# Last tile of a fused attention, recurrence and mixture-of-experts kernel: three rectifications on VectorE, a second bank for the transposes, new orders behind the last step

## What is computed

```python
a = cond_attention(x, cond)             # 16 heads, softmax over heads
x = x + linear_attention(a)             # cumulative over the heads of a token
# gated recurrence, one step per token s, all 32 batches side by side
fused = sigmoid(concat[x_s, h] @ w_W + w_b); hidden_state, output_state = split(fused, 2)
memory = x_s @ wx_W + wx_b + hidden_state * (h @ wh_W + wh_b)
h = output_state * h + (1 - output_state) * tanh(memory)
# mixture of experts over all h: 8 experts of 128 hidden units, the top 2 of 8 weighted
hidden = square(relu(einsum('nc,ecd->ned', h, w1_all)))
out    = sum over the top 2 of softmax(top-2 logits) * (hidden @ w2_all)
x = x + out
```

## Time and profile before

| | us |
|---|---|
| median of 3 runs | 379.13 |
| the 3 runs | 374.61, 379.13, 379.33 |
| the profiled execution, its own time | 374.6 |
| its span, first to last instruction | 372.9 |
| mean granted clock of TensorE in it | 0.999 |

### The profile page before, as it was taken

How to read it: one execution, slowest core, us unless ns; L and a number is a source line. 1 busy time by engine, 2 the same in 40 slices (tenths; PEclk the granted TensorE clock), 3 DMA queues, 4 the chain that set the end, 5 groups by cost and what they waited for, 6 DMA issues and landing times.

```text
span 372.9 us, 9070 instructions
## 1 busy us (share of the span) xinstructions
PE 358.7 (96%) x2528; PEld 301.9 (81%) x2528; DVE 319.2 (86%) x1160; ACT 292.6 (78%) x1136; POOL 258.2 (69%) x272
## 2 busy tenths in 40 slices
PE   6999999989999999999999999999999999999985
PEld 5689788658888888888888888888888888888873
DVE  3467897999999999999999999999999999998530
ACT  3555445568898999998999999899999989877764
POOL 4898341688777777777777777777777777777000
PEclk9999999999999999999999999999999999999999
DMA  7500000000000000000000000000000000000000
GB/s 237 202 2 0 4 0 3 0 3 1 9 10 8 10 7 11 10 11 10 10 8 10 9 9 9 8 10 8 9 8 10 8 11 9 9 9 7 10 9 14
DMA packets 7442, 6.76 MB, mean 18 GB/s; under 512 B 736, under 2 KB 6112, under 8 KB 7392
## 3 DMA queue, kind: packets, MB, share of 16 engines
q1 hardware_dynamic: 6816, 5.84, 5.0%
q10 hardware_dynamic: 576, 0.35, 0.3%
HBM read 4.09 MB, written 2.10 MB: 17 GB/s over the span
## 4 chain that ended last, share of the span: by engine, by line
PE 78%; DVE 13%; issue 4%; ACT 2%; DMA 1%; ACTq 0%; DVEq 0%; POOL 0%
PE bank L388 68%; PE bank L532 7%; DVE kvs L1095 3%; DVE mem L1135 1%; DMA XT<-in_x_t_dram 1%; PE bank L434 1%; DVE att L1104 1%; DVE rden L1087 1%; PE bank L489 1%; DVE h L1155 1%; DVE CTX L1023 1%; DVE bank L1147 1%; PE bank L481 1%; DVE bank L1140 1%; DVE ssub L1008 1%
## 5 line engine op out<-in xcount | busy, mean ns | idle before, releaser
L345 POOL TENSOR_TENSOR qc<-kvs,qn 128x512 f32<-128x512 f32 x64 | 81.4, 1273 | 53.1 <-DVE kvs L1095 52.7
L388 PEld LDWEIGHTS bank<-h,gwh 128*128 128x128 f32 x512 | 67.7, 191 | 20.8 <-DVE h L1155 16.8
L333 POOL TENSOR_TENSOR kv<-kv,qkv 128x512 f32<-128x512 f32 x64 | 80.0, 1273 | 0.2
L1095 DVE TENSOR_TENSOR_SCAN kvs<-bank,kv 128x256 f32<-128x256 f32 x128 | 79.7, 665 | 0.4 <-POOL kv L333 0.3
L840 ACT ACTIVATE hid<-bank,gw 128x128 f32<-128x128 f32 x256 | 76.8, 371 | 3.1 <-ACT gw L862 0.4
L388 PE MATMUL bank<-h,gwh 128*128 128x32 f32 x512 | 72.3, 264 | 3.5 <-DVE h L1155 3.4
L388 PE MATMUL bank<-rw,h 128*128 128x392 f32 (+2 forms) x192 | 74.9, 472 | 0.0
L388 PE MATMUL bank<-w,hsq 128*128 128x128 f32 x512 | 64.5, 279 | 0.7 <-ACT hsq L850 0.7
L388 PEld LDWEIGHTS bank<-w,hsq 128*128 128x128 f32 x512 | 59.9, 192 | 1.4 <-ACT hsq L850 1.4
L388 PE MATMUL bank<-h,whw 128*128 128x64 f32 x256 | 53.0, 289 | 0.0
L869 ACT ACTIVATE gt<-bank 128x64 f32<-128x64 f32 x128 | 29.9, 233 | 25.5 <-PE bank L388 24.3
(11 more groups left out here) (113 smaller groups left out, 704.2 us busy)
## 6 DMA issues: line engine op xcount, KB each, us to landing
out_dram<-res SPq DMA_DIRECT2D x32, 64.0 KB
XT<-in_x_t_dram SPq DMA_DIRECT2D x7, 256.0 KB, 5.3
rw<-in_rw_dram SPq DMA_DIRECT2D x1, 516.0 KB, 5.2
w<-in_w_dram SPq DMA_DIRECT2D x1, 512.0 KB, 5.9
XT<-in_x_t_dram ACTq DMA_DIRECT2D x1, 256.0 KB, 5.0
aw<-in_aw_dram SPq DMA_DIRECT2D x1, 192.0 KB, 4.2
gwx<-in_gw_dram SPq DMA_DIRECT2D x1, 128.0 KB, 4.6
gwh<-in_gw_dram SPq DMA_DIRECT2D x1, 128.0 KB, 4.4
```

What stands on the lines that cost most here:

```text
L333: pool.tensor_tensor(kv[:, a * D:b * D, :].rearrange("p (d e) h -> p d e h", d=D // 2), kv[:, D * D + a:D * D + b, :].unsqueeze(2).broadca ...
L345: pool.tensor_tensor(qc[:, a:b, :, :], kvs[:, a * D:b * D, :].rearrange("p (d e) h -> p d e h", d=D // 2), qn[:, p, a:b, :].unsqueeze(2).b ...
L388: return pe.matmul(dst, w, rhs, start=start, stop=True, skip_group_check=True)
L1095: dve.tensor_tensor_scan(flat(kvs[:, a:b, :]), scan_mask, flat(kv[:, a:b, :]), 0.0, ALU.mult, ALU.add).then_inc(kv_sum, 1)
```

## The change

Only the last tile and the finales are touched.

- DVE gets a `relu` of its own: experts 3 (half 0) and 4, 5 (half 1) of tile 31, each one `tensor_scalar` from the bank MEM into `hid`, multiplied by a column of `gw` and then the maximum with 0. It waits for `hidden` piece 1 and for `gw`, and it counts a new semaphore `hid_dv`. ACT keeps experts 0, 1, 2, 6 and 7, and `hid_sb` now counts after expert 2 and after expert 7. `hidden_T(31, half)` waits for both semaphores.
- `turned_bank`: the transposes of half 1 of tile 31 go to QKV rather than TR, and `hidden_T(31, 1)` no longer waits for `square(31, 0)`.
- `hidden(31, piece 2)` no longer waits for `hid_b`.
- PE's finale: x_rows(30), hidden_T(30, 0), hidden(31, 0), hidden_T(30, 1), experts_out(30, 0), experts_out(30, 1), hidden(31, 1), x_rows(31), hidden(31, 2), hidden_T(31, 0), hidden_T(31, 1), experts_out(31, 0), experts_out(31, 1).
- ACT's finale: x_rows_out(30), square(30, 0), square(30, 1), gate_exp(31), relu of 0 to 2, taken_sum(31), finish(30), x_rows_out(31), relu of 6 and 7, square(31, 0), square(31, 1), finish(31).
- DVE's finale: the three logit operations of tile 31, taken_inverse(30), taken_inverse(31), relu of 3, relu of 4 and 5.

```diff
--- before.py
+++ after.py
@@ -167,6 +167,7 @@
 
         l_top, l_out, l_dl, gw_done, gs_done, gr_done, mask_ok = (
             sem(n) for n in ("l_top", "l_out", "l_dl", "gw_done", "gs_done", "gr_done", "mask_ok"))
+        hid_dv = sem("hid_dv")
         hid_ps, hid_a, hid_b, hid_sb, hT_ps, hsq_sb, o_ps = sem("hid_ps"), sem("hid_a"), sem("hid_b"), sem("hid_sb"), sem("hT_ps"), sem("hsq_sb"), sem("o_ps")
 
         XTt = XT[:, :, :].rearrange("p b t -> p t b")
@@ -215,6 +216,9 @@
         def hidden_bank(t, piece):
 
             return (QKV, MEM, HID)[piece] if is_last(t) else HID
+
+        def turned_bank(t, half):
+            return QKV if is_last(t) and half else TR
 
         def out_bank(t):
             return Z if is_last(t) else OUT
@@ -519,7 +523,7 @@
                     at_least(pe, hid_sb, 2 * t)
                 if piece == 1 and not is_last(t):
                     pe.wait_ge(hid_a, t + 1)
-                if piece == 2:
+                if piece == 2 and not is_last(t):
                     pe.wait_ge(hid_b, t + 1)
                 if t == 0:
                     pe.wait_ge(pT_sb, 2 * QUADS)
@@ -527,9 +531,12 @@
 
             def hidden_T(t, half):
                 pe.wait_ge(hid_sb, 2 * t + half + 1)
-                at_least(pe, hsq_sb, 2 * t + half)
+                if is_last(t):
+                    pe.wait_ge(hid_dv, half + 1)
+                if not (is_last(t) and half):
+                    at_least(pe, hsq_sb, 2 * t + half)
                 for j in range(4):
-                    last = pe.transpose(TR[:, j * P:(j + 1) * P], hid[:, half, j, :], ident[:, :])
+                    last = pe.transpose(turned_bank(t, half)[:, j * P:(j + 1) * P], hid[:, half, j, :], ident[:, :])
                 last.then_inc(hT_ps, 1)
 
             def experts_out(t, half):
@@ -690,18 +697,18 @@
                     hidden(t - 1, q, 2)
 
             def finale():
+                x_rows(30, 0)
                 hidden_T(30, 0)
-                x_rows(30, 0)
-                x_rows(31, 1)
                 hidden(31, 1, 0)
                 hidden_T(30, 1)
                 experts_out(30, 0)
                 experts_out(30, 1)
                 hidden(31, 1, 1)
+                x_rows(31, 1)
+                hidden(31, 1, 2)
                 hidden_T(31, 0)
-                hidden(31, 1, 2)
+                hidden_T(31, 1)
                 experts_out(31, 0)
-                hidden_T(31, 1)
                 experts_out(31, 1)
 
             pipeline(pe, ramp, iteration, finale, 3)
@@ -839,15 +846,15 @@
                     col = NE + e * DE - PIECES[piece][0]
                     last = act.activation(hid[:, half, e - 4 * half, :], hidden_bank(t, piece)[:, col:col + DE], ACT.Relu,
                                           scale=gw[:, p, NE - 1 - e:NE - e])
-                    if e in (2, 5):
+                    if e in (2, 5) and not is_last(t):
                         last.then_inc({2: hid_a, 5: hid_b}[e], 1)
-                    if e in (3, 7):
+                    if e in ((2, 7) if is_last(t) else (3, 7)):
                         last.then_inc(hid_sb, 1)
 
             def square(t, half):
                 act.wait_ge(hT_ps, 2 * t + half + 1)
                 at_least(act, o_ps, 2 * t + half - 1)
-                act.activation(hsq[:, half, :], TR[:, :], ACT.Square).then_inc(hsq_sb, 1)
+                act.activation(hsq[:, half, :], turned_bank(t, half)[:, :], ACT.Square).then_inc(hsq_sb, 1)
 
             def taken_sum(t, p):
 
@@ -960,8 +967,8 @@
                     relu(t - 1, q, 1, 1)
 
             def finale():
+                x_rows_out(30)
                 square(30, 0)
-                x_rows_out(30)
                 square(30, 1)
                 gate_exp(31, 1)
                 relu(31, 1, 0, 0)
@@ -969,10 +976,8 @@
                 taken_sum(31, 1)
                 finish(30, 0)
                 x_rows_out(31)
-                relu(31, 1, 0, 2)
-                relu(31, 1, 1, 0)
+                relu(31, 1, 1, 1)
                 square(31, 0)
-                relu(31, 1, 1, 1)
                 square(31, 1)
                 finish(31, 1)
 
@@ -1103,6 +1108,17 @@
                     at_least(dve, aT_ps, t)
                 dve.tensor_reduce(att[:, :, a:b].rearrange("p h e -> p e h"),
                                   qc[:, 0:D // 2, a:b, :].rearrange("p d e h -> p e h d"), AX.X, ALU.add).then_inc(a_red, 1)
+
+            def relu(t, p, half, some):
+                experts = {(0, 2): (3,), (1, 0): (4, 5)}[half, some]
+                dve.wait_ge(hid_ps, 3 * t + 2)
+                dve.wait_ge(gw_done, t + 1)
+                at_least(dve, hT_ps, 2 * t + half - 1)
+                for e in experts:
+                    col = NE + e * DE - PIECES[1][0]
+                    last = dve.tensor_scalar(hid[:, half, e - 4 * half, :], hidden_bank(t, 1)[:, col:col + DE], gw[:, p, NE - 1 - e:NE - e], 0.0,
+                                             op0=ALU.mult, op1=ALU.max)
+                last.then_inc(hid_dv, 1)
 
             def largest_logits(t):
 
@@ -1275,11 +1291,13 @@
                     sum_heads(t + 2, 3)
 
             def finale():
-                taken_inverse(30, 0)
                 largest_logits(31)
                 drop_others(31)
                 less_top(31)
+                taken_inverse(30, 0)
                 taken_inverse(31, 1)
+                relu(31, 1, 0, 2)
+                relu(31, 1, 1, 0)
 
             pipeline(dve, ramp, iteration, finale)
 
```

## The result

| | before | after |
|---|---|---|
| median of 20 runs each, us | 376.70 | 374.62 |
| lowest run, us | 374.61 | 372.22 |
| ratio of after to before, 95% interval | | 0.9942 (0.9925 to 0.9958) |
| span of the profiled execution, us | 372.9 | 373.5 |
| mean granted clock in it | 0.999 | 0.994 |

The change makes the kernel 0.58% faster, 2.1 to 2.2 us. One of the 20 executions before took 589.21 us, slow and far out of line, and has no part in the ratio. The spans of the two profiled executions say nothing on it: all that the change touches lies behind the last h, and up to there the execution of after happened to be 2.7 us later (why is told at the end). So the measure from here on is the distance from the end of the last h (the scan of DVE that writes `h`) to the start of `finish(31)` (ACT, `res`).

A forecast was written before the change was run, and what follows sets the result against it. The finale was taken to be set by waits from engine to engine, not one engine's load. Front 0.73 + back 1.50 = 2.23 us, taken from the median 379.13, gave 376.9 us (0.994); range 372.0 to 378.8.

The forecast's parts named there:

- all four waits: PE's finale: waits for x_rows_out(30), for expert 3, for square(31, 0), and late square(31, 1); all touched by the change.
- The front: From last h to the end of piece 1: x_rows(30) and x_rows_out(30) first, hidden(31, 0) starts earlier; gain 0.73 us.
- a restart: Four PE transposes take 0.67 us after a wait, 0.44 without; hidden_T(30, 1) forecast as one, ending at 361.12.
- E: The end of piece 1, hidden(31, 1), on PE; forecast at 363.63, before 364.36.
- The back: From the end of piece 1 to finish(31): start moves from 5.27 to 3.77 us behind it; gain 1.50 us.
- Rival 1: DVE's rectifications bound the second half, at 0.55 us each; gain 1.7 us, 377.4 us; chance 0.08.
- rival 2: The front does not move, hidden_T(30, 1) or the logits being the real wait; gain 1.7, 377.4 us; chance 0.08.
- rival 3: ACT's order takes the back's gain, x_rows_out(31) delaying what queues behind; gain 1.4 to 1.7, 377.6 us; chance 0.12.
- rival 4: Slower: DVE's operation on a bank holds hidden_T(31, 1); at 1.5 us each 380.3 us; chance 0.02.
- rival 5: Another wait, the store or one unnamed, holds the end; gain under 0.5 us, about 379.0 us; chance 0.03.
- two levels, 374.6 and 379.1 to 379.3: Whole executions: one earlier run at the lower level, two at the upper; one in four put on the lower.
- The chances by 2%: Whole kernel: faster by over 2% 0.01, within 2% 0.98, slower by over 2% 0.01.

The follow-up runs named there:

- the run with the square first: Kernel after, with square(30, 0) ahead of x_rows_out(30) on ScalarE and hidden_T(30, 0) ahead of x_rows(30) on PE; 7.80 us from last h to finish(31).
- the version above: On the run with the square first, PE runs pieces 1, 2 and x_rows(31) before experts_out(30, 0), rectifications moved earlier; 7.16 us from h to finish(31), ratio to before 0.9924.
- the back alone: Kernel after with the finale's front order put back as before; VectorE's rectifications, second bank and back order stay; 8.66 us from last h to finish(31), ratio 0.9941.
- VectorE's share given back: Kernel after with experts 3, 4 and 5 back on ScalarE ahead of x_rows_out(31); 8.40 us from last h to finish(31), ratio 0.9909.
- work doubled: Kernel after with each VectorE rectification done twice, first into a spare tile nobody reads; 8.41 us from last h to finish(31).
- one bank: Kernel after with both transposed halves in TR, hidden_T(31, 1) waiting for square(31, 0) again; 8.48 us from last h to finish(31), ratio 0.9944.
- the front alone: Kernel before with only the front's reordering, no VectorE rectification, one transpose bank, old back order; 9.46 us from last h to finish(31), ratio 0.9972.
- the old one: Kernel after with the back's old order on PE and ScalarE, VectorE's rectifications and second bank kept; 9.36 us from last h to finish(31), ratio 1.0006.
- the fill: The version above plus two unread 256-column matmuls between step_memory(1, 1, 1) and step_gates(1, 1, 2) in PE's ramp; median 373.30 us, ratio to the kernel before 0.9904.

## Why the prediction was right, and where it was off

**The gain.** The forecast was 2.23 us, a ratio of 0.994; measured were 2.08 us in the profiles and 0.9942 in the times. The mechanism and its places were right, all four waits went, and the one wait that was forecast to stay, for expert 7, is the one left.

**The front.** Forecast 0.73, measured 0.69. Piece 0 ended 0.97 after h (forecast 0.94), `hidden_T(30, 1)` at 1.57 (1.52), E at 4.07 (4.03). Its inner step, that the square comes later by one ACT operation and makes the transposes a restart, was right too: 0.60 rather than 0.44 on the chain, and the run with the square first gives the 0.16 back. I counted this step as part of the forecast and did not draw the conclusion that the swap itself is a loss.

**The back.** Forecast 1.50, measured 1.38; E to `finish(31)` 3.89 us rather than 3.77. The term that was mis-sized is the last `experts_out`, "E + 1.90 to E + 3.75" with no gap. It took 1.95 rather than 1.85: `square(31, 0)` ended at E + 1.75 (forecast 1.69), only 0.17 before `hidden_T(31, 1)` did, which is too late for PE to load the first weights under the transposes. The loads show it: PE's first load for `experts_out(31, 0)` starts at 368.18, 0.05 behind the square, and in the version above it starts 0.27 before the transposes end. Six profiles give the price. Where the square ends 0.05 us before the transposes (the back alone) the 16 matmuls take 2.07, at 0.17 they take 1.95, at 0.23 (VectorE's share given back) 1.90, and at 0.44 and more (work doubled, one bank, the version above) 1.86. In the first three, lead and duration add up to 2.12 to 2.13, so the square has to be done about 2.12 - 1.86 = 0.26 us ahead to cost nothing (an estimate from these rows). The forecast had it 0.21 ahead and took that for enough. The other 0.02 are small shifts of ACT.

**VectorE's rectifications.** The estimate from the neighbouring forms was 339 ns; they take 344 ns, three in 0.87. That it came within 5 ns is partly luck, since its slope was taken from another operation. They ended at E + 0.91 (forecast 0.95), 0.31 before expert 7 (forecast 0.24). Rival 1 had the right shape: with the work doubled the loss is 0.45 and its threshold is where the rows put it. The rule of the Trainium skill (VectorE: DVE Perf Modes, The DRAIN you can't avoid) that the next operation waits for the pipe to empty is, taken alone, not what the rows show: 3 x 0.344 would be 1.03, and six in the doubled run start every 0.26. The prediction left out how that section goes on: a next operation that is not held starts earlier. With that the trace agrees. For ACT, two rectifications took 0.62 again, not the 0.68 that was estimated from the Trainium skill (ScalarE: Activation LUTs, What ACT_TABLE_LOAD costs).

**The other rivals.** The front moved (rival 2), as the front alone shows. ACT's order did not take the back's gain (rival 3): `x_rows_out(31)` started at E + 0.14 and was over before piece 2 ended. Nothing was slower (rival 4), and nothing foreign held the end (rival 5).

**The absolute time.** 376.9 us was forecast, 374.6 measured, inside the range but 2.3 off. The step that failed is the one that took the three runs of before for "two levels, 374.6 and 379.1 to 379.3" and put the median on the upper one. With 20 runs the median of before is 376.7, and the times in between are filled. 376.7 - 2.23 = 374.5 would have been the forecast from it. Three runs do not place a median that moves by 5 us between executions. The chances by 2% were right.

**What the forecast missed** is that the kernel after the change still had 0.8 us on the table, in the same few lines: its own sum held eight transposes in 1.35 us (E + 0.55 to E + 1.90; measured 1.36) that are 0.88 of work, because of the wait for expert 7, and a restart in the front. An order with the pieces first removes 0.48 there, 0.16 in front, 0.09 in the last 16 matmuls, and 0.09 because the pieces and the 16 matmuls of tile 30 take 2.87 rather than 2.96; that is 0.80 but for rounding.

## What to carry to other kernels

Behind the last step of a pipeline, write the chain as a list of hand-overs (PE to ACT to PE) and give each engine something else to do in each; an offload or an extra buffer is worth little until the order lets the engines overlap (here 0.44 and 0.52 us in the new order, 0.10 together in the old one). Let a result be ready some 0.3 us before PE wants it, not just in time (1.86 rather than 1.95 to 2.07 us for the last 16 matmuls). Issue all work that others wait for (the pieces) before work that nobody waits for (`experts_out` of the tile before). And when a change is worth 2 us in 375, measure it from a fixed event in the profile: the distance from the last h to the last operation was 7.16, 7.16 and 7.15 us in three profiles of the new order, while the executions of one kernel spread over 5 us.

## What the runs showed of the hardware

PE in the ramp of the kernel after, two waits and a later pair of matmuls (start us, us, line, operation, count, idle before):

```profile
81.98 0.63 PE L392 MATMUL bank<-h,gwh 128*128 128x32 f32 x4 [0.45 <-DVE h L1171]
84.08 0.63 PE L392 MATMUL bank<-h,gwh 128*128 128x32 f32 x4 [1.22 <-DVE h L1171]
85.63 1.34 PE L392 MATMUL bank<-awc,CTX 128*128 128x384 f32 x2
```

Stretches of the kernel after, and below of the new order's second profile (start:end, length, busy of PE, PEld, DVE, ACT, POOL, then PEclk, DMA share, GB/s):

```profile
82.00:84.00 2.00, 0.86 (x6) 0.73 (x6) 2.00 (x13) 0.85 (x4) 1.92 (x3) 1.00 0.00 0
84.00:86.00 2.00, 1.92 (x10) 1.35 (x11) 1.90 (x7) 1.56 (x8) 2.00 (x2) 0.94 0.01 4
86.00:88.00 2.00, 2.00 (x9) 1.52 (x7) 1.45 (x3) 1.50 (x8) 1.48 (x4) 0.50 0.00 0
88.00:90.00 2.00, 2.00 (x12) 1.77 (x12) 1.75 (x8) 1.60 (x9) 0.82 (x1) 0.70 0.00 0
```

```profile
84.00:86.00 2.00, 1.72 (x10) 1.32 (x11) 1.97 (x8) 1.56 (x8) 2.00 (x2) 1.00 0.01 4
86.00:88.00 2.00, 2.00 (x12) 1.39 (x12) 1.90 (x7) 2.00 (x11) 1.47 (x4) 1.00 0.00 0
```

In the first, the granted clock is at 0.50 between 86 and 88 us (1.2 rather than 2.4 GHz) although PE is fully busy there; before that PE had waited 0.45 and then 1.22 us for h, with 0.9 us of work between. In the second the clock stayed at 1.00, with the same instructions up to there and the same two waits. The waits are the same in all eleven profiles of kernels without the fill (0.45 to 0.46 and 1.21 to 1.23), the drop is not: seven have it. It is visible in the work: the second pair of 384 columns behind the wait took 1.34 us in the kernel after and 0.81 in the one before. From the end of the 1.22 us wait to the next tile's piece 0 are 7.02 us rather than 5.59, so one such stretch costs about 1.4 us. The whole recurrence says the same: from the start of its first `mem` to the start of the last h are 288.30 to 288.36 us in the five profiles without the drop (the filled one is among them) and 289.66 to 289.80 in the seven with it. In 65 executions of the kernel before that ran beside the experiments (one far outlier left out), those with a mean clock of 0.998 or more have a median of 375.7 us (26), those at 0.994 to 0.995 of 376.8 (29), those at 0.991 or less of 379.9 (10): the time goes in steps with the clock. No profile has a mean of 0.991 or less, so what those lose beyond the 1.4 us is open. One stretch at the lower clock explains 1.4 of the 2.7 us by which the last h is later in the profile of after; the other 1.3 us are there already at the first step of the recurrence (the first `mem` at 72.2 rather than 70.9 us). That start lies anywhere from 70.9 to 73.4 in the twelve profiles, ahead of all that the kernels do differently; what sets it is open.
